# First attention of a decoder: two PSUM banks shared by items and sums, with sums copied by ACT and thresholds, takes and sends in a new order

## The reference, cut to what matters

```python
q = (X @ W_Q + b_Q)      # 64 heads of 16: 4 branches of 16
k_base, v_base           # 16 heads of 16, shared by the 4 branches
q, k = (_rope(q), _rope(k))
scores = jnp.einsum('bhtd,bhsd->bhts', q, k) * ATTNSCALE
key_self = jnp.clip(jnp.sum(k * k, axis=-1), 1e-06, None)
w = jax.nn.softplus(scores / jnp.sqrt(key_self)[:, :, None, :])
w = jnp.where(causal, w, 0.0)
w = w * jax.nn.sigmoid(SCALE * w)
w = jnp.where(w < sinks, 0.0, w)
total = jnp.sum(w, axis=-1, keepdims=True) + sinks + 1e-6
out = jnp.einsum('bhts,bhsd->bhtd', w / total, v) + sinks / total * v_null
y = einsum(context of each branch, W_O) + W_O_bias, mean over the branches
```

## Time and profile before

| what | value |
| --- | --- |
| median of 3 runs | 3534.31 us (3523.79 to 3538.87) |
| the profiled execution | 3535.99 us, its span 3534.1 us |
| busy in the span | PE 84%, DVE 54%, ACT 45%, POOL 19% |
| mean granted clock of PE | 0.88 (0.83 in seven batches of this stage) |
| ACT table loads in this stage | 64, each 1283 ns |

### The profile page before, as it was taken

The page is one execution under the profiler, slowest core; times in us unless marked ns, Lnnn a source line. Parts: engine busy times, 40 slices in busy tenths (PEclk is TensorE's granted clock), DMA queues, the critical chain, the costliest instruction groups (busy, mean ns, idle before and its releaser), DMA issues. The chain is left out here.

```text
span 3534.1 us, 50554 instructions
## 1 busy us (share of the span) xinstructions
PE 2980.5 (84%) x17024; PEld 2105.8 (60%) x17024; DVE 1895.6 (54%) x4128; ACT 1589.0 (45%) x2831; POOL 684.3 (19%) x798
## 2 busy tenths in 40 slices
PE   5778878788765548999998999999998999977998
PEld 3344434444324435676662388888887777756887
DVE  3677767767773345655642144444444444445444
ACT  2767756766762123444441133333333555533221
POOL 1122112212110004444440000000000556530000
PEclk9788878878876668999995699999998999978999
DMA  2000000000000011011001000000002000010000
GB/s 91 4 3 4 0 3 3 0 3 3 0 0 28 24 53 41 22 34 28 21 20 55 3 4 3 3 3 3 3 0 79 7 3 6 6 55 33 6 6 27
DMA packets 88231, 60.88 MB, mean 17 GB/s; under 512 B 54817, under 2 KB 76705, under 8 KB 87649
## 3 DMA queue, kind: packets, MB, share of 16 engines
q1 hardware_dynamic: 88160, 59.99, 5.6%
HBM read 41.10 MB, written 8.39 MB: 14 GB/s over the span
## 5 line engine op out<-in xcount | busy, mean ns | idle before, releaser
L1760 POOL TENSOR_SCALAR x_weights<-x_weights,x_sums 128x256 f32<-128x256 f32 x256 | 232.3, 926 | 1064.5 <-DVE x_sums L1797 1064.5
L657 DVE SCALAR_TENSOR_TENSOR a_w<-a_w,a_sinks 128x384 f32<-128x384 f32 x512 | 320.6, 693 | 15.8 <-ACT a_w L491 15.8
L473 ACT ACTIVATE a_e<-psum 128x1024 f32<-128x1024 f32 x192 | 195.5, 1018 | 217.9 <-PE psum L343 184.9
L1062 POOL TENSOR_SCALAR f_weights<-f_weights,f_sums 128x256 f32<-128x256 f32 x256 | 232.7, 926 | 272.1 <-DVE f_sums L1292 272.1
L1489 ACT ACTIVATE a_weights<-psum,a_negmax 128x1024 f32<-128x1024 f32 x128 | 142.7, 1115 | 292.8 <-DVE a_negmax L1529 292.8
L1463 PE MATMUL psum<-a_v,a_turned_w 128*128 128x128 f32 x2048 | 248.3, 275 | 0.0
L340 PE MATMUL psum<-a_qT,a_kT_half 32*128 32x512 f32 x512 | 168.3, 737 | 86.3 <-DVE a_w L672 84.4
L1463 PEld LDWEIGHTS psum<-a_v,a_turned_w 128*128 128x128 f32 x2048 | 238.1, 192 | 0.0
L1529 DVE TENSOR_REDUCE a_negmax<-psum 128x1 f32<-128x1024 f32 x128 | 156.8, 1225 | 124.9 <-PE psum L123 124.1
L1220 ACT ACTIVATE f_weights<-psum,f_negmax 128x256 f32<-128x256 f32 x256 | 118.0, 473 | 214.7 <-DVE f_negmax L1286 214.7
L475 ACT ACTIVATE a_e<-a_e 128x1024 f32<-128x1024 f32 x192 | 203.2, 1058 | 6.1
(11 more groups left out here) (304 smaller groups left out, 6862.4 us busy)
## 6 DMA issues: line engine op xcount, KB each, us to landing
a_xnT<-all_xnT_all SPq DMA_DIRECT2D x16, 256.0 KB, 2.3
x_ctxT<-in_x_ctxT SPq DMA_DIRECT2D x16, 256.0 KB, 2.7
f_xnT<-all_xnT_all SPq DMA_DIRECT2D x16, 256.0 KB, 2.3
f_pv_rows<-f_pv SPq DMA_DIRECT2D x8, 512.0 KB, 3.1
f_pv_groups<-f_pv_rows SPq DMA_DIRECT2D x8, 512.0 KB
f_w<-in_f_w SPq DMA_DIRECT2D x2, 2048.0 KB, 10.1
all_x_all<-in_x SPq DMA_DIRECT2D x1, 2048.0 KB, 8.6
a_wq<-in_a_wq SPq DMA_DIRECT2D x2, 1024.0 KB, 9.3
```

Of the source, the lines that this page charges most:

```text
L473: act.activation(e[:, x, :], psS[x], ACT.Exp).then_inc(exp_done, 1)
L657: ins = dve.scalar_tensor_tensor(part, part, sinks[:, col:col + 1], part, ALU.is_ge, ALU.mult)
L1062: ins = pool.tensor_scalar(w, w, sums[:, k, h, t:t + 1], None, ALU.mult)
L1760: ins = pool.tensor_scalar(w, w, sums[:, k, h, t:t + 1], None, ALU.mult)
```

## The change

- Banks 6 and 7 both serve items and sum halves. The tables now name a bank for each item, mostly in turn, and `SUM_BANKS` one for each sum half. In PE's program `free[bank]` holds what the next user of a bank must wait for: the take of the last item in it, or the copy of the last sum.
- The sum copies move from DVE to ACT. The copy of half 0 stands in the odd step behind slot 2; the copy of half 1 in the next even step, behind slot 0 and ahead of the Silus.
- On DVE an even step has 6 points: guard 0 at point 0, thresholds 0 to 2 at points 1 to 3, guards 1 and 2 at points 4 and 5, and threshold 3 behind all of them.
- Items get new places. PE sends up to five in an even step behind slot 0's score, and one in every step behind slot 1's. All four turns are sent in step 4; ACT takes turns 0 and 1 behind the Silus and ahead of the table load, and 2 and 3 behind slot 1. The q AHEAD items are taken at (5, 0), (6, 0), (6, 5) and (7, 0), where before at (2, 5), (2, 6), (4, 1) and (4, 2). The key norm's functions move from step 3 to step 4 behind slot 2.

```diff
-EVEN_POINTS, ODD_POINTS = 7, 3
-SENT = {(0, 0): ("q", 0, HERE), (0, 1): ("q", 1, HERE), (0, 2): ("q", 2, HERE), (0, 3): ("q", 3, HERE),
...
+SENT = {0: [("regroup", 3, OLD, 7), ("q", 0, HERE, 6), ("q", 1, HERE, 7), ("q", 2, HERE, 6), ("q", 3, HERE, 7)],
...
+SUM_BANKS = {1: (7, 6), 3: (7, 6), 5: (6, 7), 7: (6, 7)}
+
+EVEN_POINTS, ODD_POINTS = 6, 3
...
+            free = {}
+
+            def sum_half(b, quad, half, bank):
...
-                wait(pe, sums_taken, 2 * n + half)
+                if bank in free:
+                    pe.wait_ge(*free[bank])
+                free[bank] = sums_taken, 2 * n + half + 1
...
-                    for sem, value in spare_free:
-                        wait(pe, sem, value)
+                    spare = psum[:, bank, :]
+                    if bank in free:
+                        pe.wait_ge(*free[bank])
...
+                def take_sums(quad, half):
+                    if quad:
+                        k, n = quad
+                        act.wait_ge(summed, 2 * n + half + 1)
+                        if half == 0:
+
+                            wait(act, regrouped, (n - 1) * 2)
+                        act.activation(sumT[:, k % 2, half * 512:(half + 1) * 512], psum[:, SUM_BANKS[(2 * k + 3) % 8][half], :],
+                                       ACT.Copy).then_inc(sums_taken, 1)
...
+                        if step % 2 == 0 and x == 0:
+                            take_sums(quad_at(b, step // 2 - 2, new, old), 1)
+                        if old and (step, x) == (4, 1):
+                            take_turned(2)
+                            take_turned(3)
...
+                        if old and (step, x) == (4, 0):
+                            take_turned(0)
+                            take_turned(1)
...
+                        if step % 2 and x == 2:
+                            take_sums(quad_at(b, (step - 3) // 2, new, old), 0)
...
-                dve.tensor_copy(sumT[:, k % 2, half * 512:(half + 1) * 512], psO).then_inc(sums_taken, 1)
...
-                        x = point if step % 2 else {0: 0, 5: 1, 6: 2}.get(point)
+                        x = point if step % 2 else {0: 0, 4: 1, 5: 2}.get(point)
...
-                        if silu_quad and 1 <= point <= 4:
+                        if silu_quad and 1 <= point <= 3:
...
-                        if summed_quad and point < 2:
-                            take_sums(summed_quad, point)
...
+                    if silu_quad:
+                        threshold(silu_quad, 3)
```

More of the change, by code:

```diff
@@ L224 @@
[L224 to L229, removed]
@@ L373, in body, with send @@
                 of = {HERE: b, AHEAD: b + 1, OLD: b - 1}
[L375 to L382, removed]
-                    bb = of[when]
-                    for sem, value in spare_free:
-                        wait(pe, sem, value)
+                free.clear()
+                if old:
+                    free.update({6: (regroup_taken, (b - 1) * REGROUPS + 3), 7: (sums_taken, ((b - 1) * QUADS + 2) * 2 + 2)})
+                elif new:
+                    free.update({6: (rot_made, b * ROTATED + 5), 7: (rot_made, b * ROTATED + 6)})
+                def send(kind, i, when, bank):
+                    bb = of[when]
+                    spare = psum[:, bank, :]
+                    if bank in free:
+                        pe.wait_ge(*free[bank])
+                    free[bank] = {"q": (rot_made, rotations(b, kind, i, when) + 1), "k": (rot_made, rotations(b, kind, i, when) + 1),
+                                  "v": (v_taken, bb + 1), "norm": (norm_taken, bb + 1),
+                                  "regroup": (regroup_taken, bb * REGROUPS + i + 1), "turn": (turn_taken, bb * 4 + i + 1),
+                                  "out": (out_taken, bb + 1)}[kind]
                     if kind in "qk":
@@ L431, in pass_through_spare @@
                         ins.then_inc(out_done, 1)
-                        spare_free = [(out_taken, bb + 1)]
                 for step in range(PAIRS_OF_HEADS):
                     quad = quad_at(b, (step - 3) // 2, new, old) if step % 2 else None
-                    for point in range(ODD_POINTS if step % 2 else EVEN_POINTS):
-                        if step % 2:
-                            x = point
-                            if quad and point < 2:
-                                sum_half(b, quad, point)
-                        else:
-                            x = {0: 0, 5: 1, 6: 2}.get(point)
-                        if x is not None and step < PAIRS_OF_HEADS - 1 and new:
+                    for x in range(SLOTS):
+                        if x < 2 and quad:
+                            sum_half(b, quad, x, SUM_BANKS[step][x])
+                        if step < PAIRS_OF_HEADS - 1 and new:
                             score_slot(b, step + 1, x)
-                        elif x is not None and step == PAIRS_OF_HEADS - 1 and ahead:
+                        elif step == PAIRS_OF_HEADS - 1 and ahead:
                             score_slot(b + 1, 0, x)
-                        if (step, point) in SENT and exists[SENT[step, point][2]]:
-                            pass_through_spare(*SENT[step, point])
+                        items = SENT.get(step, []) if x == 0 else [SENT_LATE[step]] if x == 1 else []
+                        for kind, i, when, bank in items:
+                            if exists[when]:
+                                send(kind, i, when, bank)
             over_batches(pe, body)
@@ L460, in take_turned @@
                 def take_turned(i):
+                    spare = psum[:, 6 + i % 2, :]
                     act.wait_ge(turn_done, (b - 1) * 4 + i + 1)
@@ L555, in body @@
                             ins.then_inc(ctx_ready, 1)
-                    if ahead and (step, x) == (3, 0):
+                    if ahead and (step, x) == (4, 5):
                         alone(pool, knorm_ready, b + 2, passed)
@@ L585, in _, with take_from_spare @@
             dve.wait_ge(consts, 1)
-            def take_from_spare(b, kind, i, when):
+            def take_from_spare(b, kind, i, when, bank):
                 bb = b + 1 if when == AHEAD else b
+                spare = psum[:, bank, :]
                 if kind in "qk":
```

43 lines of the change are left out of this document (17 added, 26 removed).

## The result

The changed kernel takes **3402.99 us** (median of 4 runs, 3402.72 to 3403.3), against 3535.39 for the kernel before on the same chip: a ratio of 0.9631, with a 95% interval of 0.9609 to 0.9653. That is 132 us less, where 111 had been forecast. On a second chip the ratio was 0.9607 (0.9586 to 0.9628).

A forecast was written before the change was run, and what follows sets the result against it. Hand-overs between in-order queues, no engine, bound the first attention. Pairs sum to 100.0 us a batch; 3 for hand-overs and 7.8 for clock make 110.8 against 124.5; seven batches save 96, edges 14, giving 3424 us (range 3355 to 3495).

The forecast's parts named there:

- A: Steps 0 and 1 of a batch, DVE working without a pause: 25.3 us with PE at the upper clock level.
- B: Steps 2 and 3 of a batch: 24.7 us at the upper clock level, plus 4.8 for PE's lower level.
- low stretch: PE at 1.2 GHz behind a pause, twice a batch: 4.8 us in B and 3.0 in C.
- C: Steps 4 and 5 of a batch, ACT the bound: 25.0 us at the upper clock level, plus 3.0 for the lower.
- D: Steps 6 and 7 of a batch: 25.0 us, 1.6 of it the score's wait for the next batch's last q.
- opening and end: Before and after the seven batches: three last pairs and one early at 3.4 us each, plus 4 estimated, 14 saved.
- Part 1: Sum copies from DVE to ACT: DVE loses 5.5 us of work and 15.3 of wait a batch, ACT gains 4.8.
- Parts 2 to 4: Two banks remove most idle before items; moved threshold frees slots 1 and 2 of 2.5 us; q takes leave C's chain.
- Nothing is gained: Rival: DVE's 15.3 us a batch of waiting for sums becomes a wait of ACT; 3531 us, chance 0.07.
- always at the upper level: Rival: pauses too short or too full to lower PE's clock; 103.0 us a batch, 3367 us, chance 0.15.
- Low in all four pairs: Rival: PE's clock also drops in A, adding 5 us, and D, adding 3; 118.8 a batch, 3486, chance 0.20.
- Slower: the clock stays low: Rival: PE's bursts between two banks hold the average clock at 0.60; 137 us a batch, 3622 us, chance 0.08.

The follow-up runs named there:

- v three times: The changed kernel with PE computing the v item three times over into the same bank; ratio 0.9539 to the kernel before, 3376.6 us.
- the last but one experiment: Two kernels: the changed kernel keeping only the items' new places, 0.9903; the kernel before with its fourth threshold behind the guards of slots 1 and 2, 1.0094.
- the second experiment: The changed kernel with the sum copies put back on DVE; ratio 0.9573 to the kernel before, 3388.9 us.
- the three undone at once: The changed kernel with items and sums in one bank each, sum copies on DVE and four thresholds in a row; ratio 0.9903, 3504.9 us.

## Why the prediction was right

**The bound** was read rightly: hand-overs among in-order queues, and PE's clock behind them. The whole 132 us lies in this stage.

**Pair by pair**, with what the Silu blocks of two batches show before (from 338 us on), the forecast (0.75 us of hand-overs and the price of the clock in it) and the Silu blocks above:

| pair | before us | forecast us | measured us | what differed |
| --- | --- | --- | --- | --- |
| A | 33.4, 35.1 | 26.05 | 25.97 | nothing; its one slow q is not on the chain |
| B | 32.5, 35.1 | 30.25 | 29.06 | low stretch there; it cost 4.6 us, if the 24.5 us of v three times is B without it, and 4.8 were taken |
| C | 34.1, 34.4 | 28.75 | 26.83 | low stretch there, but ACT waited 2.1 us behind it, not 3.0 |
| D | 24.0 | 25.75 | 27.38 | DVE idled 2.56 us for the output product |
| sum | 124.3, 128.2 | 110.8 | 109.2 | |

B and C came out 1.2 and 1.9 us shorter than forecast and D 1.6 us longer; that these partly cancel, and leave the sum only 1.6 us off, is luck.

**The step that failed in D** was a wait taken at nothing: the sum has 0.7 us for the take of the output product and no term for the product itself. It takes 7.07 us, all 32 of its matmuls between slot 0's score and the regroup, and ends 2.4 us after DVE has done the third threshold. No row had priced it, but the trace of the kernel before had it: DVE's wait for this product, 1.48 us behind four thresholds, is shown in the last but one experiment. With only three thresholds ahead of the take it had to grow. The new wait of the score for POOL, forecast at 1.6 us, measured 1.52. In C, ACT waited 1.76 us for slot 2 and 0.32 for the next slot 0, where 3.0 had been taken; the size was off and the mechanism right. The rest of C was priced 1.0 us too high.

**The total** came out 21 us above the forecast gain. Seven periods brought 112.7 us, not 96, since the mean period was 108.4 and not 110.8 (the first and the last, about 106 each, were not forecast apart); opening and end brought 19.6 instead of 14, whose 4 had been an estimate.

**Part 1, the sum copies**, was priced rightly (0.585 us measured, 0.6 taken) and counted as a cost on ACT's path. But the 5.5 us of work and 15.3 us of wait taken from DVE were worth nothing; the second experiment gives them back at no loss. One of the expected signs was off as well: Exp's wait for slots 0 and 1 fell to 106.1 us, not to 70. ACT's waits for sums, 22.5 us over 64 copies or 0.35 each, stayed under the 1 us each that would have spoken against the forecast.

**Parts 2 to 4.** Two banks are worth 44 us in this kernel and the moved threshold 39; the new places alone are worth 34 to the kernel before. That these do not simply add is shown by the three undone at once, 96 us instead of 63, and by the threshold, which costs 33 us where the rest is absent.

**The rivals.** "Nothing is gained" and "always at the upper level" are out by the time and by the two low windows. "Low in all four pairs" is out by pair D, which ran at 1.00, and by A, where only the third q's matmuls were slow. "Slower: the clock stays low" is out: the mean granted clock rose from 0.83 to 0.88. With items cycled through two banks the mean clock is 0.88, and with one bank each, all else as changed, it is 0.87: cycling did not lower it, and the second bank took pauses away. By the rule of the Trainium skill, "TensorE: Matmul & The Clock Gate", section "A second HAM failure mode: psum-queue depth-cycling", frequent small pauses would have cost throughput; this case does not bear that out. Its rivals were "low in all four pairs" and "slower", the second and fourth of the list, where the prediction has "third or fourth".

## What to carry to other kernels

Price each stretch by its longest chain over the in-order queues, and price every item that it waits for, above all a long one that is taken to be ready. A large wait may cost nothing: of DVE's 122 us for sums, 95 came back without any loss, while 1.5 us of idle ahead of one score lengthened its pair by 1.1. And a part of a change can gain in one arrangement and lose in another, so test it where it is to stand.

## What the runs showed of the hardware

More work for PE can save time: computing v three times over (24 matmul records a batch where there were 8), in a pause, shortened the kernel by 24 to 33 us, and in the batch shown the scores behind the pause then ran at 2.4 and not at 1.2 GHz. It is not dependable: behind a pause of 2.15 us all that followed was at the upper level in one batch of that kernel, and in the next batch, after the same work and the same pause, the second score was at the lower level; behind a pause of 2.57 us, after the same work, the first score was already so in another kernel, which gained nothing.

One threshold on DVE (four instructions) takes 2.19 us when POOL is still and 3.02 when it adds or multiplies at the same time, in the changed kernel's step 2:

```profile
303.78 3.02 DVE L670 SCALAR_TENSOR_TENSOR a_w<-a_w,a_sinks 128x384 f32<-128x384 f32 x4
...
313.79 2.19 DVE L670 SCALAR_TENSOR_TENSOR a_w<-a_w,a_sinks 128x384 f32<-128x384 f32 x4
```

```profile
304.20 0.77 POOL L547 TENSOR_TENSOR a_kT<-a_rot 128x256 f32<-128x256 f32 x1 [2.09 <-DVE a_rot L619]
305.24 0.61 POOL L551 TENSOR_TENSOR a_ksq<-a_kT 128x256 f32<-128x256 f32 x1 [0.27 <-POOL a_kT L547]
```

The two lines of POOL lie beside the first of them and none beside the second. The three thresholds of step 4 that follow one another with POOL still take 6.44 us, 2.15 each. The trace agrees with what the Trainium skill states, "GPSIMD Engine Reference", section "1. Specifications": the engine shares its SBUF interfaces with VectorE, with contention for instructions of two SBUF inputs, which these are.
